# Denominator of the attention: single third tiles of four quads added on VectorE, one product for their sum

## The reference

```
q = (x @ Wq + bq).reshape(B, N, NUM_HEADS, HEAD_DIM)
k = (y @ Wk + bk).reshape(B, M, NUM_HEADS, HEAD_DIM)
v = (y @ Wv + bv).reshape(B, M, NUM_HEADS, HEAD_DIM)
scores = jnp.einsum('bnhd,bmhd->bhnm', q, k) * scale
attn = jax.nn.softmax(scores, axis=-1)
out = jnp.einsum('bhnm,bmhd->bnhd', attn, v)
```

## Time and profile before

| what | value |
|---|---|
| median of three runs | 1385.34 us (1382.57 to 1386.74) |
| span of the profiled execution | 1383.2 us (its page gives no other time of it) |
| busy over the span: PE, VectorE, ACT, POOL | 96%, 81%, 58%, 56% |
| attention stage, 600 to 800 us: PE, VectorE, ACT, POOL | 198, 174, 142, 182 of 200 us |
| granted TensorE clock there | 1.00 |

### The profile page before, as it was taken

One profiled execution on the slowest core, in us unless ns is written; L12 is line 12 of the kernel. 1 busy time (PEld: TensorE's weight loads), 2 busy tenths in 40 slices (PEclk: granted clock), 3 DMA queues, 4 the chain that ended last, 5 costly groups with the idle time before them and its releaser, 6 DMA issues. The chain is left out here.

```text
span 1383.2 us, 39979 instructions
## 1 busy us (share of the span) xinstructions
PE 1332.2 (96%) x17098; PEld 702.8 (51%) x17098; DVE 1120.9 (81%) x1786; ACT 806.1 (58%) x1459; POOL 778.7 (56%) x320
## 2 busy tenths in 40 slices
PE   7999999998999999999999999999999999999898
PEld 4444444443555555555555555545555445566454
DVE  5778888887888888888888888888887746578895
ACT  4454444443777777776777776776777841354332
POOL 0322222122899988988998898899889100201121
PEclk9999999999999999999999999999999999999999
DMA  8568777786352122122212112211210030491000
GB/s 265 177 169 231 207 211 211 210 238 177 91 183 69 39 69 67 30 65 67 69 39 68 56 38 69 67 50 57 59 66 31 5 145 1 92 214 41 0 9 23
DMA packets 127799, 137.54 MB, mean 99 GB/s; under 512 B 44995, under 2 KB 108995, under 8 KB 125699
## 3 DMA queue, kind: packets, MB, share of 16 engines
q1 hardware_dynamic: 127622, 134.98, 34.6%
HBM read 75.70 MB, written 44.17 MB: 87 GB/s over the span
## 5 line engine op out<-in xcount | busy, mean ns | idle before, releaser
L1297 DVE TENSOR_REDUCE early<-attend_banks 128x1 f32<-128x512 f32 x952 | 612.4, 685 | 80.8 <-PE attend_banks L1042 75.6
L1261 ACT ACTIVATE attend_prob<-attend_banks 128x512 f32<-128x512 f32 x1024 | 536.0, 599 | 200.8 <-PE attend_banks L1079 198.6
L1439 POOL TENSOR_TENSOR early<-early,attend_prob 128x1024 f32<-128x1024 f32 x210 | 614.5, 2926 | 37.7 <-ACT attend_prob L1261 9.6
L1079 PE MATMUL attend_banks<-early,k_first 97*32 97x512 f16 x2560 | 258.9, 382 | 3.1 <-ACT attend_prob L1261 3.1
L1042 PE MATMUL attend_banks<-k_first,early 96*32 96x512 f16 x2272 | 235.1, 382 | 1.1 <-PEq L285 1.1
L1079 PE MATMUL attend_banks<-early,attend_k_rest 97*32 97x512 f16 x1536 | 154.1, 381 | 2.8 <-ACT attend_prob L1261 2.8
L1042 PE MATMUL attend_banks<-attend_k_rest,early 96*32 96x512 f16 x1536 | 155.8, 380 | 0.0
L1103 PE MATMUL attend_banks<-attend_prob,ones 128*32 128x128 f32 x3048 | 134.3, 272 | 3.6 <-DVE attend_recip L1309 3.6
L1092 PE MATMUL attend_banks<-attend_prob,wkv_area 128*32 128x512 f32 x1024 | 134.1, 592 | 0.0
L1092 PE MATMUL attend_banks<-attend_prob,attend_vh_odd 128*32 128x512 f32 x1024 | 133.6, 592 | 0.0
L503 POOL TENSOR_TENSOR project_w_whole<-project_grid,project_qscale 128x704 f32<-128x704 f32 x24 | 33.3, 1386 | 173.0 <-DVE project_grid L636 173.0
(11 more groups left out here) (220 smaller groups left out, 1823.6 us busy)
## 6 DMA issues: line engine op xcount, KB each, us to landing
v_scratch<-project_v SPq DMA_DIRECT2D x16, 1024.0 KB, 8.9
early<-in_ctx_dram SPq DMA_DIRECT2D x16, 768.0 KB, 6.2
k_first<-k_scratch SPq DMA_DIRECT2D x36, 256.0 KB, 3.5
k_scratch<-project_k_hi SPq DMA_DIRECT2D x64, 128.0 KB, 2.9
k_scratch<-project_k_lo SPq DMA_DIRECT2D x64, 128.0 KB, 3.1
attend_vh_odd<-v_scratch SPq DMA_DIRECT2D x8, 1024.0 KB, 5.0
wkv_area<-v_scratch SPq DMA_DIRECT2D x7, 1024.0 KB, 4.8
attend_k_rest<-k_scratch SPq DMA_DIRECT2D x24, 256.0 KB, 3.5
```

The source lines that it names most:

```text
L1079: last = nc.tensor.matmul(s_ps[c * HD:(c + 1) * HD, s_bank[n], :], key_rows[:, c * HD:(c + 1) * HD], q_stack[0:KROWS + 1, h, :], start=Tru ...
L1261: nc.scalar.activation(prob[:, q % PSLOTS, t, :], s_ps[:, s_bank[BT * q + t]], ACT.Exp, scale=SCALE).then_inc(p_ready, 1)
L1297: nc.vector.tensor_reduce(part_max[:, s, j, part:part + 1], pre_ps[:, bank], AX.X, ALU.max).then_inc(pre_read, 1)
L1439: nc.gpsimd.tensor_tensor(sums, sums, prob[:, q % PSLOTS, 0:n], ALU.add).then_inc(pool_summed, 1)
```

## The change

VectorE gets three adds per head (heads 0 to 14). The third tiles (number 2) of quads 4, 6, 8 and 10, which PE multiplied one by one, are added up in a new buffer `sum_dve`: quad 4's and 6's in quad 7, quad 8's to it in quad 9, quad 10's in quad 11, each after the second maximum of the quad. PE leaves these four products out and makes one of the sum in `denominator`, as a fourth one. ACT waits in addition for the add that reads a slot before it writes the slot again (quads 8, 10, 12 and 14). The last head stays as it was.

```diff
--- before.py
+++ after.py
@@ -861,6 +861,7 @@
             piece = carve(early)
             piece([H, T], F16)
             sum_pool = piece([2, POOL_TILES * T])
+            sum_dve = piece([2, T])
             recip = sb("recip", [P, P])
             o_out = sb("o_out", [P, 2, P])
 
@@ -886,6 +887,7 @@
             o_scaled = sem("o_scaled")
             o_stored = [sem(f"o_stored{s}") for s in range(2)]
             dve_summed = sem("dve_summed")
+            tile_summed = sem("tile_summed")
             o_in = [sem(f"o_in{k}") for k in range(DK)]
             o_high = sem("o_high")
             o_low = sem("o_low")
@@ -933,12 +935,20 @@
                 return POOL_TILES if q < 2 or q % 2 else POOL_TILES - 1
 
 
+            SUM_QUADS = (4, 6, 8, 10)
+            SUM_OPS = len(SUM_QUADS) - 1
+            SUM_TILE = POOL_TILES - 1
+            sum_op_at = {q + 1: n for n, q in enumerate(SUM_QUADS[1:])}
+            free_after = {q: max(n, 1) for n, q in enumerate(SUM_QUADS)}
+            assert all(pool_tiles(q) == SUM_TILE for q in SUM_QUADS)
+
+
             LAST_SUMMED = QUADS - 2
 
             def summed_tiles(h, q):
 
                 if not (isinstance(h, int) and h == H - 1):
-                    return pool_tiles(q)
+                    return pool_tiles(q) + (q in SUM_QUADS)
                 return DVE_TILES if q < LAST_SUMMED else 0
 
 
@@ -1118,7 +1128,12 @@
                         for t in range(TT):
                             last = nc.tensor.matmul(den_ps[t * HD:(t + 1) * HD, 0:P], ones[:],
                                                     sum_pool[:, s, n * T + t * P:n * T + (t + 1) * P],
-                                                    start=False, stop=n == tiles - 1)
+                                                    start=False, stop=n == tiles - 1 and h == H - 1)
+                    if h < H - 1:
+                        pe.wait_ge(tile_summed, SUM_OPS * (h + 1))
+                        for t in range(TT):
+                            last = nc.tensor.matmul(den_ps[t * HD:(t + 1) * HD, 0:P], ones[:],
+                                                    sum_dve[:, s, t * P:(t + 1) * P], start=False, stop=True)
                     last.then_inc(den_ready, 1)
 
                 def output(i, s, bank):
@@ -1252,6 +1267,8 @@
                             wait(act, pool_summed, Q + 1 - PSLOTS)
                         else:
                             act.wait_ge(dve_summed, min(q + 1 - PSLOTS, LAST_SUMMED))
+                        if h < H - 1 and q - PSLOTS in SUM_QUADS:
+                            act.wait_ge(tile_summed, SUM_OPS * h + free_after[q - PSLOTS])
                         if first and q == 2:
 
                             for u in range(2):
@@ -1330,6 +1347,19 @@
                     nc.vector.scalar_tensor_tensor(out=halves[:, 1], in0=chunk, scalar=WSCALE, in1=halves[:, 0],
                                                    op0=ALU.mult, op1=ALU.subtract).then_inc(mlp_split, 1)
 
+                def add_tile(i, s, n):
+
+                    h, q = 2 * i + s, SUM_QUADS[n + 1]
+                    dve.wait_ge(p_ready, BT * quad_no(i, s, q) + SUM_TILE + 1)
+                    if n == 0:
+                        wait(dve, den_ready, h - 1)
+                        first = prob[:, SUM_QUADS[0] % PSLOTS, SUM_TILE]
+                    else:
+                        dve.wait_ge(tile_summed, SUM_OPS * h + n)
+                        first = sum_dve[:, s]
+                    nc.vector.tensor_tensor(sum_dve[:, s], first, prob[:, q % PSLOTS, SUM_TILE],
+                                            ALU.add).then_inc(tile_summed, 1)
+
                 out_bank = turn_of["output"] % PRE_BANKS
                 SPLIT_AT = (2, 4, 5, 7, 8, 10)
                 O_LOW_AT = (11, 12, 13)
@@ -1381,6 +1411,8 @@
                             for j in range(TT):
                                 tile_max(s_of, part, j, TILES * h + TT * q + j,
                                          turn_of[(q, j)] % PRE_BANKS)
+                                if j == 1 and q in sum_op_at:
+                                    add_tile(i, s, sum_op_at[q])
                         if q == QUADS - AHEAD - 1 and last >= 1:
                             head_max(h + 1, 1 - s)
                         if last == 0:
```

## The result

The changed kernel takes 1408.29 us, the median of four runs (1405.41 to 1410.99), against 1386.04 of the kernel before (1382.57 to 1387.76): a ratio of 1.0159, 95% interval 1.0139 to 1.018. It is 22 us slower, where 24.5 were forecast.

The account below looks back on a forecast made before the run. PE was taken to set the attention stage's pace, with VectorE and POOL near full. 14 heads x 1.57 = 22.0 us plus 2.55 for the first gave 24.5 us slower, 1410 us; range 1399 to 1421.

Parts of the forecast that it names:

- The add waits for POOL's end and needs 0.55 behind it: VectorE's three new adds per head stand still until POOL's running add ends, then finish 0.55 us later.
- the two pairs of rows from other stages: Trace rows where POOL and VectorE operations with SBUF inputs met; VectorE ended 0.75 and 0.55 us behind POOL.
- POOL is pushed 0.27 per add: POOL's add behind each new VectorE add is held 0.55 - 0.14 - 0.14 = 0.27 us.
- The other value that the prediction weighs: From the Trainium skill's 115 ns restart: POOL held 0.52 us per add, about 32 us in all, 1417 us.
- PE's saving in quads 6, 8 and 10 is lost in waiting: PE's saved denominator products, 0.22 us each, go into waiting for VectorE's maxima, some 0.5 to 0.8 us each.
- The term of the sum: Loss per head in the attention stage: 1.57 us in 14 heads, 2.55 in the first, 24.5 us in all.
- The third maximum and the wake-up of PE: After the third add of a head, the next row maximum takes 0.61 us and PE's restart 0.06.
- The overlap of 0.08: Neighbouring row maxima on VectorE overlap by some 0.08 us, so one costs 0.61 back to back.
- the new waits: ScalarE's waits for adds before reusing slots, and PE's for POOL's later sum at the head's end: no cost claimed.
- (a): VectorE's adds run at once, 0.69 us each, and the saved products are kept: 9.9 us won, 1375; chance 0.05.
- (b): VectorE and POOL share, each slowed; an add takes some 1.3 us at once: no change, 1385; chance 0.06.
- (c): VectorE loses the race in POOL's 0.14 gap, waits one more POOL add of 3.47 us: 1545; chance 0.05.

Follow-up runs that it names:

- both removals: Two runs against the changed kernel: a row maximum in place of each add, 1378.24 us; GpSimd's adds of quads 6, 8 and 10 cut to one column, 1376.84 us.

## Why the prediction was right, point by point

- **The add waits for POOL's end and needs 0.55 behind it.** Shown in all 45 adds, and by both removals. Of the two pairs of rows from other stages the second, of the same size as the add, carried over to 0.01 us; the first, a wider operation, had 0.75.
- **POOL is pushed 0.27 per add.** Measured 0.25, 3.72 against 3.47; in head 5, from the end of POOL's add of quad 6 to that of quad 10 the changed kernel takes 12.80 us (619.71 to 632.51) where 12.26 lay before (610.42 to 622.68), 2 x 0.27, and 0.50 on the mean of heads 1 to 14. The other value that the prediction weighs, 0.52 per add and 1417 us in all, is not what the runs show. The Trainium skill (page "SBUF — State Buffer", section "A bandwidth-pool intuition that's wrong (but worth ruling out)") has the 115 ns behind that value from a DMA whose descriptors GpSimd writes, not from an add.
- **PE's saving in quads 6, 8 and 10 is lost in waiting.** PE waits three times per head, 0.7 us each by its steps; the saving itself exists (48.12 against 48.79 without the adds).
- **The term of the sum.** 1.57 us per head were forecast and 1.50 measured, 2.55 and 2.17 in the first head (49.84 - 47.67). In the stage that makes 13 x 1.50 = 19.5, 2.2 in the first head and 1.6 from head 14's first maximum to the last reciprocal: 23.3 us, against the 24.5 of the sum. The third maximum and the wake-up of PE together took 633.71 - 633.06 = 0.65 and not 0.67, and the two pushes 0.50 and not 0.54: that is 0.06 of the 0.07. The overlap of 0.08 by which the prediction has 0.61 for a maximum is in none of its rows; two of them back to back after the add take 1.27 (above) where one takes 0.67, which bears it out. Why the first head lost 0.4 less than forecast is not shown.
- **No cost of the new waits.** ScalarE waited for an add once in the whole run, for 1.5 us, and PE's weight loads for POOL's sums once, for 0.3 us.
- **The rivals.** (a), that the adds run at once, did not occur; what it would have been worth is shown by the kernel with POOL's adds cut: 1376.84, forecast at 1375. (b) and (c) did not occur either; VectorE came ahead of POOL's next add 45 times of 45, although POOL's pause is only 0.14 us.

## What to carry to other kernels

An engine with 13% of its time idle has room for an operation, but only a look at what the operation shares with its neighbours tells its price: look in the trace for the same kind of operation while the neighbour runs, and see whether its end is tied to the neighbour's end. Where two engines shut each other out, the held one stands still for the rest of what the other has under way, so the same three adds cost 0.1, 2.2 or 12.6 us per head by their place alone (in the last, part is the clock that fell behind the stand-stills); put it where the other is about to end. And a wait on the path can only be priced by the next step that depends on it, with the slack that its ring of buffers gives.

## What was not expected

A stand-still of PE of 3.17 us was followed by some 3 us at a granted clock of 0.50, while the stand-stills of the changed kernel (0.5 us idle, 1.00 granted) left the clock alone. The phase of POOL against PE, which the prediction found to repeat within 0.1 us in 14 heads, proved firm enough to place single operations shortly before the ends of its adds by hand.
